# Graph attention behind a layer norm on one core: a new beginning for the weights and new orders of work for the first four groups

## The reference, cut to what matters

```python
h = relu(layernorm(x))                                # x: (64, 128, 384), eps 1e-5, no gain
q, k, v = h @ Wq + bq, h @ Wk + bk, h @ Wv + bv       # W: (384, 384), six heads of 64
scores = q k^T / 8 + where(adj, 0, -9e15)             # per graph and head, 128 x 128
out = x + (softmax(scores) v) @ Wf + bf
```

## Time and profile before

| | |
|---|---|
| time, median of 3 runs | 478.66 us (477.88 to 484.44) |
| span of the profiled execution, first to last instruction | 475.7 us |
| time around the span, median less span | 3.0 us |
| TensorE busy | 460.9 us, 97% |
| VectorE, ScalarE, GpSimd busy | 369.5, 364.8, 299.7 us |

### The profile page before, as it was taken

One profiled execution on the slowest core, in us unless ns is written; L12 is line 12 of the kernel. 1 busy time (PEld: TensorE's weight loads), 2 busy tenths in 40 slices (PEclk: granted clock), 3 DMA queues, 4 the chain that ended last, 5 costly groups with the idle time before them and its releaser, 6 DMA issues.

```text
span 475.7 us, 12878 instructions
## 1 busy us (share of the span) xinstructions
PE 460.9 (97%) x4454; PEld 275.6 (58%) x4454; DVE 369.5 (78%) x744; ACT 364.8 (77%) x813; POOL 299.7 (63%) x300
## 2 busy tenths in 40 slices
PE   4998999999999999999999999999999999999996
PEld 2854555556556564655657465565746556464763
DVE  4799997888679587786968778695786889677955
ACT  3677998789678877777888777887878968876950
POOL 3077576777676566686656678575767657634862
PEclk9799999999999999999999999999999999999999
DMA  8138599979969799795959969595978959966796
GB/s 294 66 83 162 97 167 170 161 154 194 210 108 199 167 160 230 132 221 116 221 119 198 199 122 227 112 222 92 191 176 129 263 109 162 217 107 148 137 197 169
DMA packets 219727, 78.56 MB, mean 165 GB/s; under 512 B 199584, under 2 KB 219680, under 8 KB 219680
## 3 DMA queue, kind: packets, MB, share of 16 engines
q1 hardware_dynamic: 209056, 65.43, 70.8%
q10 hardware_dynamic: 10624, 12.53, 9.9%
HBM read 16.19 MB, written 12.58 MB: 60 GB/s over the span
## 4 chain that ended last, share of the span: by engine, by line
PE 86%; DMA 4%; SPq 4%; DVE 2%; issue 1%; ACT 1%; POOL 1%; ACTq 0%; DVEq 0%
PE ps_proj L915 24%; PE ps_proj L917 24%; PE ps_proj L916 24%; PE ps_scores L997 6%; PE ps_ctx L915 2%; PE ps_ctx L916 2%; DMA pt_parts<-probs_parts 2%; PE ps_ctx L917 2%; SPq L474 2%; SPq L466 2%; DMA x_sb<-in_x 1%; DMA ht_parts<-h_pairs 1%; SPq L456 1%; DVE masked L751 0%; PE ps_ctx L1068 0%
## 5 line engine op out<-in xcount | busy, mean ns | idle before, releaser
L543 POOL TENSOR_TENSOR probs_parts<-probs,probs_parts 128x768 f16<-128x768 f32 x64 | 105.5, 1648 | 28.2 <-ACT probs_parts L645 28.1
L630 ACT ACTIVATE probs<-masked,neg_max 128x128 f32<-128x128 f32 x384 | 118.4, 389 | 2.3 <-DVE neg_max L760 2.1
L915 PE MATMUL ps_proj<-ht_parts,w_hi 128*128 128x512 f16 (+1 forms) x309 | 111.3, 364 | 3.3 <-DVE w_lo L833 2.0
L916 PE MATMUL ps_proj<-ht_parts,w_hi 128*128 128x512 f16 (+1 forms) x309 | 111.3, 364 | 0.0
L917 PE MATMUL ps_proj<-ht_parts,w_lo 128*128 128x512 f16 (+1 forms) x309 | 111.3, 364 | 0.0
L611 ACT ACTIVATE qkt_hi<-ps_proj,bias_qk 128x512 f16<-128x512 f32 x94 | 63.6, 682 | 37.9 <-PE ps_proj L917 37.2
L549 POOL TENSOR_TENSOR ctx_parts<-ctx_sb,ctx_parts 128x384 f16<-128x384 f32 x62 | 56.8, 917 | 53.3 <-ACT ctx_parts L651 53.0
L734 DVE SCALAR_TENSOR_TENSOR qkt_lo<-ps_proj,bias_qk,qkt_hi 128x512 f16<-128x512 f32 x94 | 69.0, 740 | 22.7 <-ACT qkt_hi L611 22.7
L528 POOL TENSOR_TENSOR h_pairs<-h_sb,h_pairs 128x384 f16<-128x384 f32 x60 | 55.8, 936 | 40.7 <-ACT h_sb L602 40.5
L751 DVE SCALAR_TENSOR_TENSOR masked<-ps_scores,score_unscale,mask 128x384 f32<-128x384 f32 x128 | 72.4, 609 | 8.8 <-PE ps_scores L997 8.8
L538 POOL TENSOR_TENSOR x_bf<-x_sb,b_out 128x384 f32<-128x384 f32 x64 | 63.4, 1002 | 9.8 <-DVE y_sb L783 9.5
(11 more groups left out here) (104 smaller groups left out, 916.4 us busy)
## 6 DMA issues: line engine op xcount, KB each, us to landing
y<-y_sb SPq DMA_DIRECT2D x64, 192.0 KB, 2.7
x_sb<-in_x ACTq DMA_DIRECT2D x56, 192.0 KB, 3.1
x_sb<-in_x SPq DMA_DIRECT2D x8, 192.0 KB, 7.8
pt_parts<-probs_parts SPq DMA_TRANSPOSE x64, 4.1
ct_parts<-ctx_parts SPq DMA_TRANSPOSE x62, 3.0
adj_sb<-in_adj ACTq DMA_DIRECT2D x14, 64.0 KB, 3.2
w_raw<-in_Wq ACTq DMA_DIRECT2D x1, 576.0 KB, 4.8
w_raw<-in_Wf SPq DMA_DIRECT2D x1, 576.0 KB, 7.6
```

Of the source, the lines that this page charges most:

```text
L543: nc.gpsimd.tensor_tensor(probs_parts[b][:, 1, :], probs[b % 2][:], probs_parts[b][:, 0, :], ALU.subtract).then_inc(probs_split, 1)
L630: last = nc.scalar.activation(probs[b % 2][:, u * N:(u + 1) * N], masked[b % 2][:, u, :], ACT.Exp, bias=neg_max[b % 2][:, u:u + 1])
L915: nc.tensor.matmul(to, a_hi, b_hi, start=first, stop=False)
L916: nc.tensor.matmul(to, a_hi, b_lo, start=False, stop=False)
```

## The change

Nothing but what comes before the loop differs, and no step of groups 0 to 15 is added or dropped.

- Wq is loaded in three chunks of 128 rows, each with its own semaphore, the bias between the second and the third; its largest values are taken chunk by chunk (`reduce_first_rows`). SP loads Wk, Wv, then x of group 1, then Wf; Wf was first.
- `sum_rows(0)` stands next to the first turn; the sums have columns of their own in `ps_ctx`. Then come 4 and 3 more `keep_busy` matmuls, the second turn, and `first_q` graph by graph with the turns between.
- Low parts of Wk and Wf are made on GpSimd in two steps a chunk (`weight_scaled`, `weight_lo`); those of Wq and Wv stay on VectorE in one (`weight_rest`).
- bv @ Wf: GpSimd multiplies each chunk of Wf by bv (`bias_term`) and adds the three (`bias_sum`); TensorE sums over the rows with one f32 product by ones instead of three.
- The moments of graphs 2 and 3 of group 0 are made one by one. Wf's high and low parts are made in chunks.
- The hand-written starts become turns, and all turns up to the loop are new. The tables for groups 4 to 15 are rewritten too, but the loop's order and the order behind it come out the same on every engine, instruction by instruction.

```diff
         def row_sum(n):
-            return (ps_proj[PROJ_BANKS - 1][:, 0:1], ps_scores[:, 0:1], ps_scores[:, 1:2], ps_ctx[0][:, 0:1])[n]
+            return ps_ctx[0][:, 512 - 4 + n:512 - 3 + n]
...
-        first_parts = (slice(0, 1), slice(1, 2), slice(2, B))
+        first_parts = tuple(slice(b, b + 1) for b in range(B))
...
-            for n, w in ((3, wf), (1, wk), (2, wv)):
-                sp.dma_start(w_raw[n][:], w.rearrange("(c p) n -> p c n", p=P)).then_inc(w_loaded[n], 16)
+            sp.dma_start(w_raw[1][:], wk.rearrange("(c p) n -> p c n", p=P)).then_inc(w_loaded[1], 16)
+            sp.dma_start(w_raw[2][:], wv.rearrange("(c p) n -> p c n", p=P)).then_inc(w_loaded[2], 16)
             for b in range(B):
                 sp.dma_start(x_sb[1][:, b, :], x_v[1, :, b, :]).then_inc(x_loaded[1][b], 16)
+            sp.dma_start(w_raw[3][:], wf.rearrange("(c p) n -> p c n", p=P)).then_inc(w_loaded[3], 16)
...
+            def bias_term(group, c, i):
+                if c == 0:
+                    pool.wait_ge(bias_loaded, 16)
+                    pool.wait_ge(w_loaded[3], 16)
+                nc.gpsimd.tensor_scalar(bias_terms[c][:], w_raw[3][:, c, :], bias_raw[:, 2, c:c + 1], None, ALU.mult)\
+                    .then_inc(bias_term_ready, 1)
+
+            def bias_sum(group, c, i):
+                pool.wait_ge(bias_term_ready, C + c)
+                nc.gpsimd.tensor_tensor(bias_terms[0][:], bias_terms[0][:], bias_terms[c + 1][:], ALU.add)\
+                    .then_inc(bias_term_ready, 1)
+
+            def weight_scaled(group, item, i):
+                n, c = divmod(item, C)
+                pool.wait_ge(scale_step, SCALE_STEPS * (n + 1))
+                if item >= C:
+                    pool.wait_ge(w_split[n - 1], c + 1)
+                nc.gpsimd.tensor_scalar(w_scaled[c][:], w_raw[n][:, c, :], w_scale[:, n:n + 1], None, ALU.mult)\
+                    .then_inc(w_scaled_ready[n], 1)
+
+            def weight_lo(group, item, i):
+                n, c = divmod(item, C)
+                pool.wait_ge(w_hi_ready[n], c + 1)
+                pool.wait_ge(w_scaled_ready[n], c + 1)
+                nc.gpsimd.tensor_tensor(w_lo[n][:, c, :], w_scaled[c][:], w_hi[n][:, c, :], ALU.subtract)\
+                    .then_inc(w_split[n], 1)
...
-            act.dma_start(w_raw[0][:], wq.rearrange("(c p) n -> p c n", p=P)).then_inc(w_loaded[0], 16)
+            wq_v = wq.rearrange("(c p) n -> p c n", p=P)
+            act.dma_start(w_raw[0][:, 0, :], wq_v[:, 0, :]).then_inc(wq_loaded[0], 16)
+            act.dma_start(w_raw[0][:, 1, :], wq_v[:, 1, :]).then_inc(wq_loaded[1], 16)
             act.dma_start(bias_raw[:], biases).then_inc(bias_loaded, 16)
+            act.dma_start(w_raw[0][:, 2, :], wq_v[:, 2, :]).then_inc(wq_loaded[2], 16)
...
+            def sum_rows(group, n, i):
+                pe.wait_ge(rows_reduced[n], C if n == 0 else 1)
+                if n < 2:
+                    pe.wait_ge(bias_summed, 1)
+                if n >= 1:
+                    pe.wait_ge(scale_step, SCALE_STEPS * (n - 1) + 1)
...
             def project_bias(group, item, i):
-                pe.wait_ge(bv_ready, 1)
-                pe.wait_ge(w_loaded[3], 16)
-                for c in range(C):
-                    last = nc.tensor.matmul(ps_ctx[0][:, 0:H], bv_cols[:, c, :], w_raw[3][:, c, :],
-                                            start=c == 0, stop=c == C - 1)
-                last.then_inc(bv_projected, 1)
+                pe.wait_ge(bias_term_ready, 2 * C - 1)
+                pe.wait_ge(scale_step, SCALE_STEPS * 3 + 1)
+                nc.tensor.matmul(ps_ctx[0][:, 0:H], plain_ones[:], bias_terms[0][:], start=True, stop=True)\
+                    .then_inc(bv_projected, 1)
```

More of the change, by code:

```diff
@@ new lines @@
+    4: {
+        "load": (-550, -440, -420, -400), "load_mask": (-450,), "statistics": (-510, -410, -310, -300),
+        "aggregate": (-290,), "inverse_deviation": (-160,), "shift": (-250,), "normalize": (-210, -180, -150, -140),
+        "normed_lo": (-100, -80, -60, -50), "transpose_normed": (-70, -40), "additive_mask": (-70,),
+    },
+    5: {
+        "load": (-10250, -10230, -10070, -10050), "load_mask": (-10190,),
+        "statistics": (-10120, -10010, -9605, -8910),
+    },
+    6: {
+        "load_mask": (-20090,),
+    },
@@ L122 @@
     },
     13: {
-        "load": (-13387, -12684, -11466, -10307), "load_mask": (-1896,),
-        "statistics": (-11123, -10679, -9776, -8555), "aggregate": (-7633,), "inverse_deviation": (-8866,),
-        "shift": (-6381,), "normalize": (-5548, -3980, -3387, -2829), "normed_lo": (-5004, -3732, -3730, -2991),
-        "transpose_normed": (-2887, -2059), "project_qk": (2084, 2085, 2086, 2088, 2089, 4366),
-        "qk_hi": (2386, 3038, 3275, 3277, 3278, 4669), "qk_lo": (1366, 4654, 4691, 4974, 4975, 4977),
@@ new lines @@
+        "shift": (-48590,), "normalize": (-48700, -48680, -48660, -48650),
+        "normed_lo": (-49260, -49250, -49240, -49230), "transpose_normed": (-49370, -49350),
+        "project_qk": (-49020, -49010, -49000, -48990, -48980, -48970),
+        "qk_hi": (-48560, -48540, -48510, -48490, -48480, -48470),
+        "qk_lo": (-48380, -48360, -48350, -48340, -48320, -48310), "project_v": (-48890, -48860, -48830, -48780),
+        "values_hi": (-48350, -48300, -48280, -48250), "values_lo": (-48170, -48120, -48090, -48070),
```

515 lines of the change are left out of this document (262 added, 253 removed).

## The result

The changed kernel takes 484.24 us in the median of 19 runs, the kernel before 479.0 in 19 runs beside them; the ratio is 1.0111 (95% interval 1.0089 to 1.0133). I had said 476.0 and a range up to 480.2. The profiled execution has a span of 481.4 us, 5.7 more than the 475.7 before.

The account below looks back on a forecast made before the run. TensorE, busy 460.9 of 475.7 us, bounds the kernel; only the first 41 us can improve. Gain of 3.5 us at group 1 less 0.8 for handovers is 2.7; 478.66 - 2.7 = 476.0 us, range 473.0 to 480.2 (about 8 in 10).

Parts of the forecast that it names:

- the price of one-input work on GpSimd: Scaling a 384-column weight chunk on GpSimd: taken as 0.65 us, bounded by 0.29 and 1.0 us.
- hidden, with 1.1 us to spare: Wk's third low part on GpSimd: done at 21.2 us, needed by project_qk(0,3) at 22.3.
- nearly hidden: VectorE's shift(1) waits for GpSimd until 24.2 us; Wv's first low part at 25.0, project_qk(0,4) ends at 24.9.
- Rival B: GpSimd sets the pace, each scaling and product at 1.0 us; little gain left, 478.3 us; chance 0.14.
- hidden by 0.1 us: Value bias: GpSimd's sums end at 26.3 us, the scale at 26.4, TensorE comes to project_bias at 26.5.
- Rival D: Wv's low parts on VectorE and GpSimd's bias sums exclude each other: up to 1 us, 477.0 us; chance 0.05.
- my 36.8: Start of project_qk(1,0), group 1's first projection: 36.0 us by the walk, plus 0.8 for handovers.
- The last about when the whole did: Wq loaded in thirds: the last third lands about when the whole load did, 5.6 us.
- From there the change moves work between engines that have slack, and TensorE stays full: After weigh_values(0,0): work moves between engines with slack, TensorE stays full, so the 2.7 us gain is kept.
- the first side of the walk: Beginning up to the end of the first q: project_qk(0,3) at 21.0 us instead of 22.10, gain 1.1 us.
- rival C: Groups 0 to 3: a later transfer is missed and TensorE waits; one whole miss gives 480.9 us; chance 0.13.
- rival A: Clock stays up through first_q 0, project_qk(1,0) 1.2 us better: 474.0 us, or 473.2 without handover loss; chance 0.13.

Follow-up runs that it names:

- const_scale: Changed kernel with the constant 2.0 instead of Wk's and Wf's scales in GpSimd's scaling; 485.53 us, a single time.
- u_bias: Changed kernel with the value bias back on TensorE as three f32 projections, no products or sums for it on GpSimd; 479.48 us, 1.0016 of the kernel before.
- u_lo: Changed kernel with Wk's low parts back on VectorE, one instruction a chunk; 479.08 us, 1.0002 of the kernel before.
- best: Changed kernel with Wq in one load, value bias on TensorE and Wk's low parts on VectorE; 477.54 us, 0.9970 of the kernel before.
- both: Changed kernel with the value bias back on TensorE and Wk's low parts back on VectorE together; 479.45 us, 1.0001 of the kernel before.
- Late_join: Changed kernel up to about 41 us, then the kernel before's sequence, with Wf's low parts on VectorE; 484.76 us, 1.0142 of the kernel before.
- one_load: Changed kernel with Wq in one load again, ahead of the biases, reductions still in thirds; 481.97 us, 1.0072 of the kernel before.
- wf_vec: Changed kernel with Wf's low parts back on VectorE, nothing else; 482.31 us, 1.0068 of the kernel before.
- best_wf: Changed kernel with Wq in one load, value bias on TensorE, and Wk's and Wf's low parts on VectorE; 475.16 us, 0.9940 of the kernel before.
- no_keep: Changed kernel without the seven new keep-busy matmuls; 484.25 us, 1.0110 of the kernel before.

## Why the prediction was wrong

**The step that failed** is the price of one-input work on GpSimd: "the one-input select on 128 columns, 0.29. The select is the nearest in kind: with 0.1 for the start (the memset of four columns) it costs 1.5 ns a column, 0.67 us for 384; I take 0.65", and the bound "from above it is bounded by the two-input f32 row, 1.0 us". It costs 1.24. That one input costs no more than two was an assumption that no row bore out, and with it the range was too narrow as well. Six such instructions stand ahead of inverse_deviation(1): 6 x 0.59 = 3.5 us. My 24.2 for the shift becomes 27.7, and it started at 27.48. With it failed what I had built on the price: the third low part of Wk, "hidden, with 1.1 us to spare", held TensorE up for 1.39 us, and the wait for Wv's, "nearly hidden", for 2.43 us and then 0.61 and 0.53. The Trainium skill's page "GPSIMD Engine Reference", section "Engine selection", which puts one-input work on GpSimd at roughly line rate and from which I gave 0.32 us plus the start, is contradicted by the rows of the changed kernel (1.24) and of const_scale (1.16).

**Rival B** named the right mechanism and the right sign of the deviation, but with the same bound, so it ended at 478.3. By its own walk, 1.24 instead of 1.0 is 6 x 0.24 = 1.4 us more on the wait at shift(1): 479.7, and with D's 2.2 us 481.9. (In the recorded walk at 1.0 us, Wv's first low part is there at 25.0 + 6 x 0.35 = 27.1 by my own terms, not at 26.8.) I had called the value bias "hidden by 0.1 us" and the new wait "nearly hidden", and had not asked what twice the price would do to both at once. The undo of either part (u_bias, u_lo) brings the median ratio to within 0.2% of the kernel before, since both stand in one queue ahead of one instruction, and both together give no more.

**Rival D** held fully and was priced too low. "Each of Wv's three low parts (0.55 us) holds up a bias sum or is held by one of 1.0 us: up to 1 us". The shift has two inputs in SBUF as well, and each handover waits for a whole instruction of 1.0 to 1.2 us: 0.94 for 0.16, and 3.06 for 1.67, 2.2 us together. The rule of the Trainium skill (page "SBUF — State Buffer", section "Who interferes with whom") is borne out by four kernels: with sums beside them 0.94 and 3.06 (changed, u_lo), without 0.16 and 1.67 (u_bias, best).

**The first loss as a whole** is these two and a term that I had put at nothing, the clock. I had project_qk(1,0) at 36.0, plus 0.8 for handovers: 36.8, set by a transfer. It was 41.63, 4.8 us late, and no wait for a transfer stands before it: TensorE works without a pause from 31.47 on. Until then it had waited 1.39 us for Wk's third low part and 3.57 us for Wv's three. Because of these waits it also worked at the lower clock from 31.05 to 34.4. What that cost shows beside u_lo, where the same steps, from the third chunk of the first value projection to project_qk(1,0), run at a granted clock of 1.00:

```profile
28.57 0.34 PE L995 MATMUL ps_scores<-w_hi,ht_parts 128*128 128x384 f16 x1 [0.52 <-DVE w_lo L950]
...
37.27 0.38 PE L995 MATMUL ps_proj<-ht_parts,w_hi 128*128 128x512 f16 x1
```

That is 8.70 us, and 10.16 in the changed kernel (31.47 to 41.63): 1.5 us for the clock. Together 6.4 us; without them TensorE would have been there at 35.2, 1.6 us ahead of my 36.8, hence 4.8. Behind the 3.57 us stand, on VectorE, the late shift (3.3 us, 27.48 for 24.2) and the exclusion (2.2 us). U_lo, which has the exclusion still, stands at 37.27, u_bias, which has neither bias sums nor products, at 37.50, and both at 36.08. Late_join confirms the price: its order is the changed kernel's up to there, but its clock fell at 29.0 and was back at 32.4, so that less of the work met it, and the same steps take 9.10 us (31.56 to 40.66). That the clock fell because of the waits is read from the traces only (it stays at 1.00 in u_bias, u_lo and both).

**"The last about when the whole did"** was wrong too: the third chunk of Wq was reduced at 8.28, the whole at 5.52. My own queue of VectorE work (8.3 for the scale) hid part of it, the scale came at 9.9, and one_load showed 1.3 us of it on TensorE and on the shift alike. Of the shift's 3.3 us against my walk it explains little, since GpSimd began at 16.15, where I had 15.8.

**"From there the change moves work between engines that have slack, and TensorE stays full"** failed for the second loss of 2.4 us. GpSimd's 6.5 us for Wf cost 2.0 of them (wf_vec; best_wf against best: 1.5). What the other 0.4 us and the 1.2 us behind the loop are isn't settled; by the medians, 5.2 us slower, rather 0.7 than 1.2 us is left behind the loop. In the changed kernel TensorE waits 0.78 us for a low part of queries at 419 and 1.86 us for pt_parts at 471, and the kernel before has two waits too, of 0.76 and 1.39. That the loop's steps keep their turns while GpSimd's start later relative to them is a guess that I didn't try.

**Right**: the first side of the walk, project_qk(0,3) at 21.0 (20.91), but by luck in part, since two misses met: the scale of Wq came 1.6 us late and the first projection at 12.64 instead of 11.4, and the clock that I had taken for the lower one was 1.00. Right too were one matmul for project_bias; the loop as it was (167.84 us from (4,0) to (10,0) in both); and that no transfer would be missed on the path (rival C): the longest wait for one ahead of the loop's start is 0.62 us. Of rival A the mechanism came, against my forecast: the clock stayed up through first_q. Of its worth 0.6 us came at project_qk(0,3) and nothing that shows in the time (no_keep). The walk that gave 1.2 us for it had TensorE's own work as the limit, where it was ACT's and VectorE's. Its recorded times are also too low by 0.8: 39.5 - 34.8 = 4.7 us is already the gain with no handover lost, so the rival stood at 474.8 or, with none lost, 474.0, and the range should have begun there; the result lies on the other side.

## What to carry to other kernels

When work is moved to an engine that has "slack", price it with the dearest row of that engine, not the nearest in kind, then walk the queue to the one short instruction that others wait for: six instructions that were each 0.6 us dearer than thought made a critical wait of an inverse root that takes 1.04 us. Count what shares a resource as one cost: two moves each hidden by 0.1 to 1 us were not hidden together, and undoing either one got nearly everything back. A wait can cost more than its length: here the clock fell behind it and took another 1.5 us. A gain on one engine's clock or a chunked load is worth little until the trace shows that what it speeds up ends last.
